# A graph layer's edge kernel: the first group's k rows computed from gathered x rows, not gathered from the table

## The reference, cut to what matters

```python
h  = jnp.maximum(_layernorm(x, axis=-1), 0.0)
eq = h @ Wq + bq
ek = h @ Wk + bk
e  = edge_attr_256 @ We + be
m  = jax.nn.relu(eq[dst] + ek[src] + e)
ft = jax.ops.segment_sum(m, dst, num_segments=6250)
return x + (ft @ Wr + br)
```

## Time and profile before

| | us |
|---|---|
| median of 3 runs | 1135.0 |
| lowest and highest | 1132.82, 1135.22 |
| the profiled execution | 1135.05 |
| its span | 1132.9 |
| TensorE busy in the span | 1093.3 (97%) |
| VectorE busy | 938.9 (83%) |
| ScalarE busy | 879.3 (78%) |
| GpSimd busy | 842.9 (74%) |

### The profile page before, as it was taken

How to read it: one execution, slowest core, us unless ns; L and a number is a source line. 1 busy time by engine, 2 the same in 40 slices (tenths; PEclk the granted TensorE clock), 3 DMA queues, 4 the chain that set the end, 5 groups by cost and what they waited for, 6 DMA issues and landing times.

```text
span 1132.9 us, 28566 instructions
## 1 busy us (share of the span) xinstructions
PE 1093.3 (97%) x9114; PEld 1077.4 (95%) x9114; DVE 938.9 (83%) x1371; ACT 879.3 (78%) x1560; POOL 842.9 (74%) x939
## 2 busy tenths in 40 slices
PE   8859999999999999999999999999999999999998
PEld 7849999999999999999999999999999999998997
DVE  7758888888888888888888888888888888878787
ACT  6847787788787878887877877887877877877774
POOL 7667777777777777777777777777777777777773
PEclk9969999999999999999999999999999999999999
DMA  9769898898988898898999989889898988987882
GB/s 321 213 212 299 273 288 276 284 286 279 285 280 279 281 286 285 276 284 276 286 283 275 290 280 281 284 280 285 281 281 278 288 284 276 285 278 247 272 252 87
DMA packets 171122, 309.09 MB, mean 273 GB/s; under 512 B 30817, under 2 KB 117358, under 8 KB 171038
## 3 DMA queue, kind: packets, MB, share of 16 engines
q1 hardware_dynamic: 130878, 199.05, 52.7%
q0 software_dynamic: 39888, 108.97, 34.0%
q10 hardware_dynamic: 272, 0.26, 0.1%
HBM read 281.20 MB, written 26.95 MB: 272 GB/s over the span
## 4 chain that ended last, share of the span: by engine, by line
POOL 33%; DVE 20%; issue 18%; DMA 15%; PE 11%; ACT 1%; SPq 1%; POOLq 0%; DVEq 0%; ACTq 0%
POOL k_rows L710 33%; DVE p_edge L1147 18%; DMA k_rows<-k_table,idx 14%; PE p_edge L1299 5%; PE p_sum L1299 3%; PE p_sum L1397 1%; DVE hT_lo L1178 1%; PE p_edge L1376 1%; PE p_turn L1319 1%; DMA q_table<-m_hi 1%; DMA ft<-in_x 0%; PE p_turn L1386 0%; PE p_turn L1299 0%; POOL hn L648 0%; POOLq L308 0%
## 5 line engine op out<-in xcount | busy, mean ns | idle before, releaser
L710 POOL DMA_INDIRECT k_rows<-k_table,idx x815 | 779.3, 956 | 248.6 <-issue 186.6
L1299 PE MATMUL p_edge<-we_hi,edge_hi 128*128 128x256 f32 x1662 | 476.1, 286 | 26.6 <-DMA q_win<-q_table 13.5
L1299 PE MATMUL p_edge<-we_lo,edge_hi 128*128 128x256 f32 x1662 | 465.2, 280 | 0.0
L1299 PE MATMUL p_edge<-we_hi,edge_lo 128*128 128x256 f32 x1662 | 464.6, 280 | 0.0
L1147 DVE TENSOR_TENSOR p_edge<-p_edge,k_rows 128x1024 f32<-128x1024 f32 x208 | 256.1, 1231 | 165.8 <-DMA k_rows<-k_table,idx 134.4
L1299 PEld LDWEIGHTS p_edge<-we_hi,edge_hi 128*128 128x128 f32 x1662 | 314.6, 189 | 39.1 <-issue 30.2
L846 ACT ACTIVATE m_hi<-p_edge 128x1024 fp32r<-128x1024 f32 x208 | 213.6, 1027 | 159.0 <-DVE p_edge L1147 159.0
L1299 PEld LDWEIGHTS p_edge<-we_lo,edge_hi 128*128 128x128 f32 x1662 | 315.3, 190 | 0.0
L1299 PEld LDWEIGHTS p_edge<-we_hi,edge_lo 128*128 128x128 f32 x1662 | 313.0, 188 | 0.0
L1125 DVE TENSOR_TENSOR edge_lo<-edge,edge_hi 128x1024 fp32r<-128x1024 f32 x208 | 253.8, 1220 | 2.6 <-ACT edge_hi L795 2.6
L1156 DVE SCALAR_TENSOR_TENSOR m_lo<-p_edge,m_hi 128x1024 fp32r<-128x1024 f32 x208 | 253.4, 1218 | 0.3 <-ACT m_hi L846 0.3
(11 more groups left out here) (148 smaller groups left out, 1095.2 us busy)
## 6 DMA issues: line engine op xcount, KB each, us to landing
edge<-in_edges SPq DMA_DIRECT2D x208, 512.0 KB
rel_row<-rel_table SPq DMA_DIRECT2D x208, 96.0 KB
q_win<-q_table SPq DMA_DIRECT2D x416, 48.0 KB
k_rows<-k_table,idx POOLq DMA_INDIRECT x815
q_table<-hn SPq DMA_DIRECT2D x46, 256.0 KB, 3.8
pre<-in_x SPq DMA_DIRECT2D x55, 128.0 KB, 3.2
out_rows<-pre SPq DMA_DIRECT2D x55, 128.0 KB, 1.7
k_table<-k_rows SPq DMA_DIRECT2D x23, 256.0 KB, 4.2
```

The lines of the kernel that those rows point to most:

```text
L710: nc.gpsimd.indirect_dma_start(out=k_rows[:, slot, j, :], out_offset=None, in_=k_table, in_offset=bass.IndirectOffsetOnAxis(ap=offsets, ax ...
L1299: ins = nc.tensor.matmul(target, a(h), b[:, h, :], start=(start and h == 0 and n == 0), stop=(stop and h == HALVES - 1 and n == 2))
```

## The change

The four tiles of group 0's edges are treated like two more pairs of node blocks (`EDGE_PAIRS` = 2, pairs 25 and 26; `ALL_PAIRS` = 27; a seventh norm part of 4 blocks).

- GpSimd gathers the x rows of group 0's source nodes straight from the input x (`gather_x`), two tiles in step 15 and two in step 17, into the space of edge slot 3 (`x_edge`). Their statistics, centring, turning, splitting and product with Wk follow behind the 25 pairs and behind the first q product; ScalarE writes the k rows into slot 0 of `k_rows` where the gathers would have put them. The gathers after the pairs start with group 1.
- The chain of the windows on VectorE moves from steps 19 to 23 to behind the pair loop; in its place, in the steps, come the splits of later weights and the row statistics of the four new blocks. `rel_idx` moves behind the first q rows.
- VectorE clears 7 parts of `ft` behind its first two `edge_low`, in place of 3; GpSimd clears 3 behind the pairs, in place of 2 within them and 5 behind.
- The highest and lowest targets, the range stores and loads, and small constants move by one to three steps; `dst_idx` is loaded three steps earlier. The statistics are spread over one more pair (`STATS_OF_PAIR`).
- ScalarE's queue issues the stores of pair 24's two k blocks. The load of edge group 3 goes behind the windows and behind the turning of pair 26.

```diff
-NORM_PARTS = ((0, 4), (4, 8), (8, 16), (16, 28), (28, 40), (40, NODE_BLOCKS))
+EDGE_PAIRS = TILES // 2
+ALL_PAIRS = NODE_PAIRS + EDGE_PAIRS
+ALL_BLOCKS = 2 * ALL_PAIRS
+NORM_PARTS = ((0, 4), (4, 8), (8, 16), (16, 28), (28, 40), (40, NODE_BLOCKS), (NODE_BLOCKS, ALL_BLOCKS))
+NODE_PARTS = len(NORM_PARTS) - 1
...
-VECTOR_CLEARS = 3
-SLOT_CLEARS = 2
+STATS_OF_PAIR = (4, 4) + (3,) * 8 + (4, 3, 3)
+VECTOR_CLEARS = 7
...
+        x_edge = edge[:, UNROLL - 1].rearrange("p h e -> p (h e)").rearrange("p (t d) -> p t d", d=D)
...  SyncE
-                    sp.wait_ge(s_prep, PREP_STEPS - 1)
-                    sp.dma_start(rel_table.rearrange("(p c) e -> p c e", c=CHUNKS), rel_g[:]).then_inc(s_rel, 16)
...
+            sp.wait_ge(s_prep, PREP_STEPS)
+            sp.dma_start(rel_table.rearrange("(p c) e -> p c e", c=CHUNKS), rel_g[:]).then_inc(s_rel, 16)
...
-            for u in range(2, UNROLL):
-                load_edge(0, u)
+            load_edge(0, 2)
...
-            sp.wait_ge(s_hT, NODE_PAIRS)
+            sp.wait_ge(s_hT, ALL_PAIRS)
             load_next_x(0)
+            load_edge(0, 3)
...  GpSimd
+            def gather_x(tiles):
+                if tiles[0] == 0:
+                    pool.wait_ge(s_src, 16)
+                for j in tiles:
+                    nc.gpsimd.indirect_dma_start(
+                        out=x_edge[:, j, :], out_offset=None, in_=x,
+                        in_offset=bass.IndirectOffsetOnAxis(ap=src_idx[:, 0, j:j + 1], axis=0),
+                        engine_sem=s_wrote,
+                    ).then_inc(s_xedge, 16)
...
-                if i == 12:
+                if i == 13:
                     mean(4)
-                if i == 13:
+                if i == 14:
                     variance(4)
-                if i == 14:
                     mean(5)
                     variance(5)
+                if i == 15:
+                    gather_x(range(2))
                 if i == 16:
                     refine(4)
+                    later_constants()
                 if i == 17:
-                    later_constants()
+                    gather_x(range(2, TILES))
...
-            for c in pool_clears[SLOT_CLEARS:]:
+            mean(NODE_PARTS)
+            pool_centre(NODE_PAIRS)
+            variance(NODE_PARTS)
+            for i in range(NODE_PAIRS + 1, ALL_PAIRS):
+                pool_centre(i)
+            refine(NODE_PARTS)
+            for c in pool_clears:
                 clear(pool, nc.gpsimd, c)
...
-            for u in range(UNROLL):
+            for u in range(1, UNROLL):
...  ScalarE
             copy_k(NODE_PAIRS - 2)
+            for i in range(NODE_PAIRS, ALL_PAIRS):
+                centre(i, 1)
+            deviation(NODE_PARTS)
             copy_k(NODE_PAIRS - 1)
             for v in range(FIRST_PAIRS):
                 first_q_high(v)
+            for i in range(NODE_PAIRS, ALL_PAIRS):
+                h_hi(i)
+            for i in range(NODE_PAIRS, ALL_PAIRS):
+                copy_k(i)
...  VectorE
-                if i == 19:
-                    widest_span()
-                if i == 20:
-                    order_of_windows()
...
+                if i == 23:
+                    for k in range(NODE_BLOCKS, ALL_BLOCKS):
+                        row_statistics(k)
+            widest_span()
+            inverse(NODE_PARTS)
+            order_of_windows()
+            window_starts()
+            for c in range(CHUNKS):
+                group_nodes(c)
+            window_table()
...
-                dve.wait_ge(s_rows[slot], 16 * TILES * body + 16 * tiles)
+                if isinstance(n, int) and n == 0:
+                    after(dve, s_kcopy, ALL_BLOCKS - 1)
+                else:
+                    dve.wait_ge(s_rows[slot], 16 * TILES * (body if slot > 0 else body - 1) + 16 * tiles)
...
             for v in range(FIRST_PAIRS):
                 first_q_low(v)
+            for i in range(NODE_PAIRS, ALL_PAIRS):
+                h_lo(i)
+            dve.wait_ge(s_lanes, 16)
+            nc.vector.tensor_tensor(rel_idx[:], dst_idx[:], win_f[:].unsqueeze(2).to_broadcast(
+                [LANES, GROUPS, TILES]), ALU.subtract).then_inc(s_prep, 1)
             for u in range(2):
                 edge_low(0, u)
...  TensorE
             for v in range(FIRST_PAIRS):
                 first_q_product(v)
+            after(pe, s_kcopy, NODE_BLOCKS - 1)
+            for i in range(NODE_PAIRS, ALL_PAIRS):
+                turn_h(i)
+            for i in range(NODE_PAIRS, ALL_PAIRS):
+                k_product(i)
```

More of the change, by code:

```diff
@@ L215, in gnn_program @@
         s_lanes = sem("lanes_loaded")
+        s_src = sem("source_numbers_loaded")
         s_wk = sem("k_weights_loaded")
@@ L233, in gnn_program @@
         s_blank = sem("bias_operands_blank")
-        s_x = [sem(f"x_loaded_{c}") for c in range(len(NORM_PARTS))]
+        s_x = [sem(f"x_loaded_{c}") for c in range(NODE_PARTS)]
+        s_xedge = sem("x_rows_of_first_edges_gathered")
         s_bias = sem("bias_rows_added")
@@ L401, in store_k @@
                     sp.dma_start(k_blocks[2 * v], k_out[:, i % NRING, 0:D]).then_inc(s_kstore[i % NRING], 16)
-                elif i == NODE_PAIRS - 1:
-                    for j in range(2):
-                        after(sp, s_kcopy, 2 * i + j)
-                        sp.dma_start(k_blocks[2 * v + j], k_out[:, i % NRING, j * D:(j + 1) * D])\
-                            .then_inc(s_kstore[i % NRING], 16)
                 else:
@@ L764, in copy_k @@
                 act.wait_ge(s_rstd, max(p for p, f in enumerate(FIRST_PAIR) if f <= i) + 1)
-                after(act, s_kp, i)
-                k_stored(act, i - NRING)
+                after(act, s_kp, i if i < NODE_PAIRS else i + 1)
+                if i < NODE_PAIRS:
+                    k_stored(act, i - NRING)
+                elif i == NODE_PAIRS:
+                    for v in range(NODE_PAIRS - NRING, NODE_PAIRS):
+                        k_stored(act, v)
                 if i == EMPTY_STEP:
@@ L773, in copy_k @@
                         after(act, s_kp, i + j)
-                    nc.scalar.activation(k_out[:, i % NRING, j * D:(j + 1) * D], k_place(i, j),
+                    target = (k_out[:, i % NRING, j * D:(j + 1) * D] if i < NODE_PAIRS else
+                              k_rows[:, 0, 2 * (i - NODE_PAIRS) + j, :])
+                    nc.scalar.activation(target, k_place(i, j),
                                          ACT.Copy, scale=at(rstd, 2 * i + j)).then_inc(s_kcopy, 1)
+                    if i == NODE_PAIRS - 1:
+                        after(act, s_kcopy, 2 * i + j)
+                        act.dma_start(k_blocks[2 * PAIR_ORDER[i] + j], k_out[:, i % NRING, j * D:(j + 1) * D])\
+                            .then_inc(s_kstore[i % NRING], 16)
             def first_q_high(v):
@@ L913, in _ @@
             act.wait_ge(s_shift, 1)
-            act.wait_ge(s_lanes, 32)
+            act.wait_ge(s_src, 16)
             for u in range(FIRST_IDX, FIRST_IDX + 3):
```

101 lines of the change are left out of this document (44 added, 57 removed).

## The result

The changed kernel takes 1143.06 us (median of 5 runs, 1141.49 to 1144.78) against 1135.16 of the kernel before in the same runs: a ratio of 1.0074, 95% interval 1.0062 to 1.0086, so 7.9 us more. The profiled execution took 1143.27 us with a span of 1141.4.

A forecast was written before the change was run, and what follows sets the result against it. GpSimd's gathers set the time from about 145 us, but VectorE's first additions decide the start. Additions 4.7 us late (weight 0.92) and gathers 2.8 (0.08) gave 4.5 us on 1135.0: 1139.5 us; own range 1136.5 to 1142, full range 1134.5 to 1143.5.

The forecast's parts named there:

- GpSimd's saving: Group 0's four gathers after the pairs go: 5.0 us saved on GpSimd, predicted to turn into a wait.
- the sum: Shift of the end: 0.92 times the additions' delay plus 0.08 times the gathers' delay, 4.5 us later.
- a: Delay of VectorE's line of k row additions: 3.4 us at the first addition plus 1.3 for a low clock, 4.7.
- the second price: TensorE waits some 3.5 us for group 0's m_lo after group 1; its clock then falls, costing 1.3 us.
- the locked stage: Long middle part to the end, paced by GpSimd's gathers: predicted 5.0 us a group as before, no added loss.
- x gathers that block the pairs: Rival: the first x gather stalls GpSimd in pair 15, pairs end near 63; about 1143 us, chance 0.18.
- What goes out of the pairs: Index chain leaves the node pairs: 4.5 us of stalls go, plus 0.7 net gain; last pair's product ends at 59.6.
- What is late next: VectorE's serial chain behind the pairs: pair 25's h_lo at 68.3, both products at lower clock, ScalarE's copies end at 74.4.
- TensorE's own start: Group 0's product, behind the table stores: starts 82.1 to 84.5, ends 86.5 to 90.7, beside or ahead of VectorE's 90.8.
- g: Delay of GpSimd's line of gathers: gather(4) starts at 92.5 behind the first addition, +2.8 us.
- The cancelling case: Rival: TensorE keeps its full clock in pairs 25 and 26, first addition 1.1 us late; about 1136 us, chance 0.2.
- The faster case: Rival: GpSimd's head start reaches the end, needing VectorE ready by 83; about 1130.5 us, chance 0.12.

The follow-up runs named there:

- the saving alone: The kernel before, with group 0's four gathers from the table left out and nothing else changed: 1134.32 us, ratio 0.9998.
- the three runs with the clears alone: Changed kernel, VectorE clearing three pieces and GpSimd the four taken over behind its twelve gathers: 1416.72, 1419.70, 1416.11 us; ratios 0.9973, 0.9966, 0.9970 to the kernel before.
- the one with the register: Changed kernel, VectorE reading the number of passes before its first low parts instead of behind its clears: 1420.15 us, ratio 0.9982 to the kernel before.
- the run with the second group kept warm: Changed kernel with 30 idle TensorE transposes ahead of the product of group 2: 1139.57 us, ratio 1.0039 to the kernel before.
- the run with three clears: Changed kernel with VectorE clearing three pieces instead of seven and GpSimd the other nine: 1134.99 us, ratio 1.0015 to the kernel before.
- the one with edge pairs and early table: Changed kernel with early q store and windows, three VectorE clears, idle transposes ahead of pair 25 and group 0: 1133.15 us, ratio 0.9992 to the kernel before.

## Why the prediction was right or wrong

The direction held, and so did the mechanism up to the first addition: GpSimd's saving turns into a wait, and VectorE's longer chain delays the additions. The size did not hold: 4.5 us were forecast and 7.9 came (1139.5 against 1143.06). The step that failed is the sum, "a = 3.4 + 1.3 = 4.7" with nothing behind it. By the lateness of the additions in the two traces three terms are short:

- the first addition, 4.1 us in place of 3.4: a register read of 1.1 us had no term (part of it was offset by a chain 0.3 us faster);
- the second price, 2.3 in place of 1.3;
- the locked stage, 2.0 in place of nothing ("from then 5.0 us a group as before").

Together they are 3.7 us, about the 3.6 that were missing. The first two are shown by runs; why the third exists stays open. That 1143.06 lies within 1134.5 to 1143.5 is luck: the forecast's own range ended at 1142, and the rest of it was room for x gathers that block the pairs, which they did not.

*GpSimd's saving is a wait.* Right: 9.76 us ahead of group 4's gather where about 10 was named, and 0.9998 for the saving alone.

*What goes out of the pairs.* Right: no stall remained where the 3.11 and 2.77 us stood; ScalarE's refine wait took 1.66 us. The gain was put too high: the last node pair's product ended at 60.7, not 59.6. It did no harm, since VectorE's chain, which waits for the root, is what comes last.

*What is late next.* Right in each row, to 0.5 us: root and reciprocal at 62.05 (61.5) after 2.19 us of standing (2), pair 25's product at 68.78 after 4.23 us (68.3, 4.7) with a granted clock of 0.50, edge_hi at 74.78 (74.4), first clear at 80.89 (80.9), last clear's end 90.53 (90.8).

*The first addition.* "The addition starts at 90.9": it started at 91.65. The chain was right and 0.3 us faster than said; the read of the pass count behind the clears, 1.1 us, had no term. In the kernel before it stands in the program at the same place, inside the 8.37 us of idle time, and can't be seen there. With it the chain gives 90.5 + 1.1.

*TensorE's own start.* Predicted 82.1 to 84.5 for the start of group 0's product and 86.5 to 90.7 for its end. It started at 82.61, with the table's load back issued at 79.85, and was done by 88.26. "VectorE decides" is right. The profile's releaser spoke against it and misled me in two expectations; the three runs with the clears alone and the one with the register speak for it.

*A second price.* Taken at 1.3, it measured 2.3. The wait was sized well (3.93 against 3.5), the low stretch after it was not. The granted clock was 0.50 from 94.0 to 100.8, and from 95.55 on TensorE worked at the half rate, 5.2 us in place of 2.6 to 3.4. The error is to take the length of the low stretch from the one gap of 2.77 us, which was shorter and left the clock at 0.50 for 3.4 us.

*The sum's weights.* a = 6.4 and g = 3.9 give 0.92 x 6.4 + 0.08 x 3.9 = 6.2 at the meeting; it was 5.66 at group 12 and 6.38 at group 14. Good to 0.6. GpSimd's line isn't free either: it waited again at groups 6 and 7.

*No term: the locked stage.* After group 14 the sum lets nothing happen. Yet the median is 7.9 late, and the additions go from 6.38 to 8.42, 5.01 us a group in place of 5.00. In the trace after, 14 gathers from 145 us on took longer than 1.02 us (5.1 us of excess in all) against 6 (2.6 us) before; 11 of the 14 and 4 of the 6 started just behind the start of VectorE's edge_lo. A step like this is in the run with the second group kept warm (1.6 us, 13 long gathers), and 2.4 us in the profiled execution of the run with three clears (13), which was 3.4 us above its own median; the six other runs on chips at 1134 us had 4 to 8, the one with edge pairs and early table among them (8, and 0.6 us lost). So the edge pairs alone don't make it. Nor is it sure that it is all the kernel's: in single executions of the kernels on these chips groups 14 to 207 took from 963.6 us (without the first gathers, a kernel as fast as before by its median) to 967.8, with 965.3 before and 967.4 after. Why the changed kernel has it isn't settled: its three further traces come from chips where this stage has another bound.

What makes a gather long is in the traces, and it is finer than the prediction's "falls on VectorE's edge_lo". Over the ten traces on chips at 1134 us, all 142 gathers from 84 us on that started 0.15 to 0.85 us behind the start of an edge_lo ended 2.03 to 2.05 us after that start, which is 0.8 us behind its end. The 1817 that started between 0.2 us ahead of it and 0.02 us behind took 0.94 to 1.06 us, though they run beside it for most of their length. In the trace after, GpSimd's gather and VectorE's edge_lo:

```profile
147.53 1.22 DVE L1158 TENSOR_TENSOR edge_lo<-edge,edge_hi 128x1024 fp32r<-128x1024 f32 x1
147.79 1.77 POOL L727 DMA_INDIRECT k_rows<-k_table,idx  x1 [0.30 <-issue]
```

0.26 us behind, and 1.77 long. In the locked stage those gathers that meet an edge_lo mostly start with it or 1.0 us and more behind its start, and take 0.95; one that slips in between costs up to 0.9 us.

*The rivals.* The x gathers did not block the pairs: the first took 1.21 us and started with its usual 0.30 behind the instruction before. (The Trainium skill, GPSIMD Engine Reference, section 2.1 "Instruction dispatch", has about 6 us for the first call into a freshly loaded kernel; nothing of the kind is in this trace, and the measurement decides.) The cancelling case failed on the clock, as argued. The faster case asked for VectorE to be ready by 83. With three clears it was ready at 85, the additions started at 86.30, and the time was about that of before; but GpSimd began its gathers at 71.60 there, so its head start was not put to the test. With the edge pairs and the early table VectorE was ready at 83.5, GpSimd waited for nothing, and the time was that of before: most of the head start had gone into the pairs' own work on GpSimd, which reached group 4 at 88.50, 1.2 us ahead of before.

## What to carry to other kernels

Work taken off the engine that sets the pace is worth nothing until the stage that it paces can begin: ask first what the first consumer waits for, and then what stands 1, 3 and 5 us behind that. Idle time ahead of a step hides not only work but also small reads and waits that show up once the cover is gone, so add them from the code, not from the trace. And when a wait is put down to an engine, look for another instruction that waits for the same result, and see when that one started.

## What the runs showed of the hardware

- A gather that started 0.15 to 0.85 us behind the start of VectorE's edge_lo (1.22 us, two SBUF operands) always ended 2.03 to 2.05 us after that start (142 gathers in ten traces): 1.89 us for the earliest, 1.18 for the latest. One that started with it or up to 0.2 us ahead took its usual 0.95 (at most 1.06, 1817 gathers).
- A register read from a tile's value ahead of VectorE's loop took 1.1 us between two instructions (1.09 to 1.11 in six traces, 0.1 without it). The profile puts it down to TensorE in four of the six, to a DMA in one and to nothing in one.
- From the issue of the q table's store to that of its load back it took 6.9 to 8.9 us in the seven traces at 1134 us in which GpSimd's gathers had started 1.3 to 4.9 us ahead of the store, and 5.2, 5.2 and 5.9 us in the three in which they started with it or behind it (in one of them four gathers were issued beside it). On the slower chips it was 7.7 to 9.9 against 5.4.
- TensorE's granted clock was 0.50 for 3.4 us, from 1.4 us behind the end of a wait of 2.77 us; and for 6.8 us, from 1.6 us ahead of the end of a wait of 3.93, 5.2 of them with TensorE at work.
- The same kernel took 1134 us on some chips and 1420 on three others, with equal lengths of VectorE's and ScalarE's instructions, 221 in place of 279 GB/s in the middle stage, and 85 to 93 us of TensorE's stops there that the profile names no cause for, against none; the change costs 0.7% on the first and nothing that can be told on the others.
